# Fetch of edge rows written out with constant index addresses, three buffers, 41 turns beside one stage and 15 beside the next

## The reference, cut to what matters

```python
edge_index = stack([src, dst])
h = maximum(layernorm(x), 0);  x = x + L0(h, edge_index, W1, b1, W2, b2, W3, b3)   # three gcn layers 16-64-64-16
h = maximum(layernorm(x), 0);  x = x + L1(h, edge_index, ...)                      # 16-256-256, messages, 512-256-16
h = maximum(layernorm(x), 0);  x = x + L2(h, src, dst)                             # degree-scaled sum over edges
h = maximum(layernorm(x), 0);  x = x + L3(h, edge_attr_16, ...)                    # attention over edges

def L3(feat, efeat, W_msg, b_msg, W_attn, b_attn, src, dst):
    w_m = (efeat @ W_msg + b_msg).reshape(E, 16, 16)
    w_a = (efeat @ W_attn + b_attn).reshape(E, 16, 16)
    e1, e2 = w_m * feat[src][:, :, None], w_a * feat[src][:, :, None]
    attn = softmax of e2 over the edges of one target, for each of the 256 channels
    return segment_sum(e1 * attn, dst).sum(axis=1)
```

## Time and profile before

| | us |
|---|---|
| median of three runs | 3270.18 |
| profiled execution, its own time | 3269.55 |
| span of the profiled execution | 3267.7 |
| `layer0`, 745.5 to 1026.9 | 281.4 |
| `layer1_nodes`, 1026.9 to 1146.0 | 119.1 |
| `layer1_sum`, 1146.0 to 1385.5 | 239.5 |
| attention, from 1518 on | 1749 |

### The profile page before, as it was taken

How to read it: one execution, slowest core, us unless ns; L and a number is a source line. 1 busy time by engine, 2 the same in 40 slices (tenths; PEclk the granted TensorE clock), 3 DMA queues, 4 the chain that set the end, 5 groups by cost and what they waited for, 6 DMA issues and landing times. The chain is left out here.

```text
span 3267.7 us, 39524 instructions
## 1 busy us (share of the span) xinstructions
PE 2426.8 (74%) x7146; PEld 911.0 (28%) x7146; DVE 2494.0 (76%) x4298; ACT 1861.9 (57%) x7322; POOL 1358.8 (42%) x1220
## 2 busy tenths in 40 slices
PE   0888887785982689975688888888887888788740
PEld 0111111133551445533222222222222222222210
DVE  5999999943012445411699999999999999999977
ACT  2888888700000111110788788788878877887820
POOL 3000000006664400002676666666666766666503
PEclk8555556677975799987566766676677667667665
DMA  1000000002332554420122222222222222222113
GB/s 16 0 0 0 0 0 0 0 3 78 89 85 73 144 182 147 143 79 18 30 65 74 64 69 77 65 69 71 71 65 65 77 65 69 77 65 69 56 61 86
DMA packets 122244, 201.37 MB, mean 62 GB/s; under 512 B 55143, under 2 KB 76536, under 8 KB 116320
## 3 DMA queue, kind: packets, MB, share of 16 engines
q1 hardware_dynamic: 84192, 170.52, 15.0%
q0 software_dynamic: 38016, 30.45, 5.4%
HBM read 72.73 MB, written 128.17 MB: 61 GB/s over the span
## 5 line engine op out<-in xcount | busy, mean ns | idle before, releaser
L1463 POOL DMA_INDIRECT hs<-h_table,gix x880 | 1064.3, 1209 | 492.8 <-issue 265.7
L1555 ACT ACTIVATE e<-wps,hs 128x32 f32<-128x32 f32 x5632 | 1009.9, 590 | 201.1 <-PE wps L1487 160.0
L1487 PE MATMUL wps<-w_edge,ef 18*128 18x512 f32 x1760 | 729.7, 895 | 336.9 <-DVE e L1593 187.4
L1509 PE MATMUL slot_sums<-e,ident 128*128 128x512 f32 x1056 | 572.6, 700 | 9.7 <-DVE e L1658 9.7
L357 PE MATMUL acc<-q_hot,lo_hot 128*128 128x400 bf16 x1200 | 469.0, 495 | 132.8 <-DVE q_hot L327 70.3
L1487 PEld LDWEIGHTS wps<-w_edge,ef 18*128 18x128 f32 x1760 | 217.9, 248 | 812.9 <-DVE e L1593 337.2
L311 ACT ACTIVATE lo_hot<-lane,loT 128x128 bf16<-128x128 f32 x1200 | 353.7, 387 | 19.4 <-PE acc L357 19.2
L336 DVE TENSOR_TENSOR edges<-acc,edges 128x400 f32 x600 | 338.5, 564 | 22.6 <-PE acc L357 17.0
L1509 PEld LDWEIGHTS slot_sums<-e,ident 128*128 128x128 f32 x1056 | 230.6, 227 | 377.8 <-issue 367.3
L1593 DVE TENSOR_TENSOR e<-wps,hs 128x1024 f32<-128x1024 f32 (+1 forms) x220 | 314.6, 1430 | 26.9 <-PE wps L1487 26.9
L327 DVE TENSOR_SCALAR q_hot<-qcol,qT 128x400 bf16<-128x400 bf16 x1200 | 325.9, 313 | 5.3 <-issue 4.1
(11 more groups left out here) (305 smaller groups left out, 1979.8 us busy)
## 6 DMA issues: line engine op xcount, KB each, us to landing
rows_state<-states SPq DMA_DIRECT2D x44, 1280.0 KB, 4.6
rows_shift<-shifts SPq DMA_DIRECT2D x44, 640.0 KB, 3.0
edges_order<-got SPq DMA_DIRECT2D x56, 256.0 KB, 2.6
got_order<-edges_order SPq DMA_DIRECT2D x56, 256.0 KB, 2.9
ef_order<-efT SPq DMA_DIRECT2D x56, 256.0 KB, 3.0
hs<-h_table,gix POOLq DMA_INDIRECT x880
ef<-ef_order SPq DMA_DIRECT2D x44, 320.0 KB, 3.0
msg<-m_parts SPq DMA_DIRECT2D x10, 480.0 KB, 4.9
```

The lines of the kernel that those rows point to most:

```text
L1463: nc.gpsimd.indirect_dma_start(out=hs[u][:, s, :], out_offset=None, in_=d["h_table"], in_offset=bass.IndirectOffsetOnAxis(ap=gix[u][:, s:s ...
L1487: nc.tensor.matmul(wps[:, bank, :], ef[u][k:k + KM, g * P:(g + 1) * P], w[k:k + KM, :], start=True, stop=True).then_inc(a_mult, 1)
L1509: ins = nc.tensor.matmul(sums[:, (u + g) % 2, :], ident[:, :], e[u][:, g * SLOTS + c, :], start=(c == 0), stop=(c == SLOTS - 1))
L1555: ins = nc.scalar.mul(e[u][:, s, at], wps[:, bank, at], hs[u][:, s, f:f + 1])
```

## The change

The fetch counts single turns instead of pairs. `gather` and `store` take a Python number `n`, so that all 56 turns are written out. The gathers read their addresses directly from `start`; the tile `ix`, the copy into it and its two semaphores are gone. There are three buffers `got` with a semaphore pair each, turn `n` in buffer `n % 3`. 41 turns lie beside `layer0`, and 15 beside `layer1_nodes`, three in each of its five rounds. The loops of POOL (L684) and SP (L674) are gone.

```diff
-FETCH0 = GORDER // TURN // 2 - 5
+FETCH0 = GORDER // TURN - 15
...
+    TURNS = GORDER // TURN
+    RING = 3
...
-    def gather(self, pool, i, v):
-        nc = self.nc
-        nc.gpsimd.tensor_copy(self.ix[v][:, :], self.start[:, bass.ds(i * (2 * TURN) + v * TURN, TURN)]
-                              ).then_inc(self.y_idx, 1)
-        pool.wait_ge(self.y_idx, i * 2 + (v + 1))
-        pool.sem_inc(self.y_go, 1)
+    def gather(self, pool, n):
+        nc, v, k = self.nc, n % self.RING, n // self.RING
+        if k:
+            pool.wait_ge(self.gathered[v], 16 * TURN * k)
+            pool.wait_ge(self.stored[v], 16 * k)
         for g in range(TURN):
             nc.gpsimd.indirect_dma_start(
                 out=self.got[v][:, g, :], out_offset=None, in_=self.edge_rows,
-                in_offset=bass.IndirectOffsetOnAxis(ap=self.ix[v][:, g:g + 1], axis=0)).then_inc(self.gathered[v], 16)
+                in_offset=bass.IndirectOffsetOnAxis(ap=self.start[:, n * TURN + g:n * TURN + g + 1], axis=0)
+            ).then_inc(self.gathered[v], 16)
...
+    def store(self, sp, n):
+        v, k = n % self.RING, n // self.RING
+        sp.wait_ge(self.gathered[v], 16 * TURN * (k + 1))
+        sp.dma_start(self.edges_order[n * P:(n + 1) * P, :],
                      self.got[v][:, :, :].rearrange("p g n -> p (g n)")).then_inc(self.stored[v], 16)
...
-                with sp.Fori(0, FETCH0) as i:
-                    for v in range(2):
-                        fetch.store(sp, i, v)
+                for n in range(FETCH0):
+                    fetch.store(sp, n)
...
-                for v in range(2):
-                    fetch.gather(pool, 0, v)
-                with pool.Fori(1, FETCH0) as i:
-                    for v in range(2):
-                        fetch.gather_again(pool, i, v)
+                for n in range(FETCH0):
+                    fetch.gather(pool, n)
...
-                    for v in range(2):
-                        fetch.store(sp, FETCH0 + c, v)
+                    for v in range(3):
+                        fetch.store(sp, FETCH0 + 3 * c + v)
...
-                for c in range(ROUNDS):
-                    for v in range(2):
-                        fetch.gather_again(pool, FETCH0 + c, v)
+                for n in range(FETCH0, fetch.TURNS):
+                    fetch.gather(pool, n)
```

More of the change, by code:

```diff
@@ L418 @@
 class Fetch:
-    PAIRS = GORDER // TURN // 2
+    TURNS = GORDER // TURN
+    RING = 3
     def __init__(self, nc, ctx, io, keep, d, sem):
         self.nc, self.edge_rows, self.start, self.edges_order = nc, io["edge_rows"], keep["start"], d["edges_order"]
[L425 to L429, removed]
-    def gather(self, pool, i, v):
-        nc = self.nc
-        nc.gpsimd.tensor_copy(self.ix[v][:, :], self.start[:, bass.ds(i * (2 * TURN) + v * TURN, TURN)]
-                              ).then_inc(self.y_idx, 1)
-        pool.wait_ge(self.y_idx, i * 2 + (v + 1))
-        pool.sem_inc(self.y_go, 1)
+        self.got = [ctx.enter_context(nc.sbuf_tensor(f"got{v}", [P, TURN, SLOTS * KE], F32)) for v in range(self.RING)]
+        self.gathered = [sem(f"y_gather{v}") for v in range(self.RING)]
+        self.stored = [sem(f"y_stored{v}") for v in range(self.RING)]
+    def gather(self, pool, n):
[3 more added lines that the diff above has]
+            pool.wait_ge(self.stored[v], 16 * k)
         for g in range(TURN):
@@ L440, in gather, with wait_stored @@
                 out=self.got[v][:, g, :], out_offset=None, in_=self.edge_rows,
-                in_offset=bass.IndirectOffsetOnAxis(ap=self.ix[v][:, g:g + 1], axis=0)).then_inc(self.gathered[v], 16)
[L443 to L452, removed]
+                in_offset=bass.IndirectOffsetOnAxis(ap=self.start[:, n * TURN + g:n * TURN + g + 1], axis=0)
[4 more added lines that the diff above has]
+        sp.dma_start(self.edges_order[n * P:(n + 1) * P, :],
                      self.got[v][:, :, :].rearrange("p g n -> p (g n)")).then_inc(self.stored[v], 16)
-    def wait_stored(self, sp, pairs):
-        for v in range(2):
-            sp.wait_ge(self.stored[v], 16 * pairs)
+    def wait_stored(self, sp, turns):
+        for v in range(self.RING):
+            sp.wait_ge(self.stored[v], 16 * len(range(v, turns, self.RING)))
 def edge_groups(nc, io, keep, d, sem):
@@ L833, in _ @@
                                      parts[:, :, :, f * P:(f + 1) * P]).then_inc(n_dm, 16)
-                    for v in range(2):
-                        fetch.store(sp, FETCH0 + c, v)
+                    for v in range(3):
+                        fetch.store(sp, FETCH0 + 3 * c + v)
                 sp.wait_ge(n_dh, 16 * ROUNDS)
                 sp.wait_ge(n_dm, 32 * ROUNDS)
-                fetch.wait_stored(sp, fetch.PAIRS)
+                fetch.wait_stored(sp, fetch.TURNS)
             @block.gpsimd
             def _(pool):
-                for c in range(ROUNDS):
-                    for v in range(2):
-                        fetch.gather_again(pool, FETCH0 + c, v)
+                for n in range(FETCH0, fetch.TURNS):
+                    fetch.gather(pool, n)
             @block.tensor
```

## The result

| us | before | after | ratio, 95% interval |
|---|---|---|---|
| median, five runs each | 3271.28 (3267.5 to 3275.73) | 3235.63 (3233.88 to 3239.89) | 0.9892 (0.9878 to 0.9907) |
| profiled execution | 3269.55 | 3234.76 | |
| `layer0` | 281.35 | 237.91 | |
| `layer1_nodes` | 119.08 | 129.05 | |
| from `layer1_sum` on | 2121.7 | 2120.3 | |

The forecast was 3229. The span is 34.9 us shorter: -43.4 in `layer0`, +10.0 in `layer1_nodes`, -1.4 behind. The first term is the forecast one, the second is more than three times its size (+2.8 was forecast). That is the larger finding, and it comes last among the experiments.

A forecast was written before the change was run, and what follows sets the result against it. The fetch, on POOL's issue rate, was taken to hold `layer0` open for nearly 45 us. Profiled 3269.55 - 43.6 (`layer0`) + 2.8 (last round of `layer1_nodes`) = 3228.8, predicted 3229 us, range 3221 to 3238.

The forecast's parts named there:

- The first term: Border of `layer0` and `layer1_nodes`: DVE's idle time of 44.82 us becomes 1.23, so -43.6 us.
- the case that had 0.68: Whole kernel: the forecast holds as summed, 3224 to 3233 us; chance 0.68.
- the worst last round: Last round of `layer1_nodes`, upper bound: stretch 3.1 us and a slowly landing store, +6.8 us; total 3232.8.
- The copies go, five turns move: POOL in `layer0`: 0.75 us per turn saved, 164 gathers instead of 184, last gather ends at 960.6.
- DVE is late next, nothing else near: End of `layer0`: DVE's arithmetic is last at about 983.4, the fetch having 16.6 us to spare.
- The third buffer costs nothing in `layer0`: Fetch in `layer0`: a buffer has two turns, 10 us, to land, be stored and land again; costed at nothing.
- The last round, +2.8: Last round of `layer1_nodes`: twelve gathers instead of eight delay the third store, +2.8 us, bounds +0.6 and +6.8.
- The port rule: Last round of `layer1_nodes`: two two-input DVE passes could each hold a gather up to 1.49 us; term +4.0.
- The rounds keep their length: `layer1_nodes`: the sum allows no change in the rounds, which took 77.4 us from first to last.
- The rival on round lengths: `layer1_nodes`: clock changes make the rounds -7.7 or +2.6 us, total 3221.1 or 3231.4; chance 0.08 for over 4 us.
- The written-out list starves POOL: POOL in `layer0`: bringing in written-out gathers costs +0.6 us each, total 3311 us; chance of slower 0.04.
- the forecast of a faster kernel: Whole kernel: sign of the change, faster 0.95, same 0.01, slower 0.04.

The follow-up runs named there:

- e5: Changed kernel with two buffers instead of three; 3480.51 us in one run, on the chip where the kernel before takes 3345.8.
- e3: Changed kernel with 44 turns beside `layer0` and 3, 3, 3, 3, 0 in the rounds of `layer1_nodes`; 3228.93 us, before 3272.6 on that chip.
- e6: Changed kernel with the old split, 46 turns beside `layer0` and two per round; 3493.38 us, before 3345.8 on that chip.
- e7: Changed kernel with 44 turns beside `layer0`, then 3, 3, 3, 3, 0, without the last turn's gathers; 3456.16 us, ratio 1.048 to before.
- a_after_again: The changed kernel without any edit, timed again on the chip of 3298.2; 3449.75 us, ratio 1.0451 to the kernel before.
- e12: Changed kernel with copy, wait and increment per turn, 43 turns beside `layer0`, then 3, 3, 3, 4, 0, last turn's gathers omitted; 3287.79 us, ratio 0.9965 to before.
- e4: Changed kernel, each turn first copying its four addresses into a tile the gathers read, with a wait; 3236.31 us, before 3272.6 on that chip.
- e11: Changed kernel with each turn's address copy, the wait and a separate semaphore increment behind it put back; 3291.12 us, before 3298.2 on that chip.

## Why the prediction was right, and where not

The total was right by its range of 3221 to 3238, on the chip where it was measured. It lies outside the 3224 to 3233 of the case that had 0.68: the profiled execution got 34.8 us shorter where -40.8 was forecast. The first term carries the forecast. The terms of `layer1_nodes` were 7 us too small together, and 1.4 came back in the stages behind, which the sum took as unchanged. The total stayed in the range only because its upper bound lay 5 us above the worst last round, for the clock's spread; that part was luck.

- **The copies go, five turns move; -43.6 us.** Right: -43.4. POOL's busy time is 162.1 (forecast 162.5), the last gather ends at 957.95 (960.6). The 0.75 us per turn was the right size but not the copy's: the copy is 0.2 of it, and only copy and increment together make the rest. Taking both away at once hid that.
- **DVE is late next, nothing else near.** Right, with 0.53 us of idle time for the forecast 1.23; that its last sum ends 0.8 us later (982.93 for 982.15) offsets this. The third buffer costs nothing in `layer0`, and gives little there (e5).
- **The last round, +2.8.** The mechanism is right, the third store behind two, but the term is +6.1, near its upper bound of 6.8. Landing was taken as 4.3 us from round 1 and is 6.7 (+2.4): the last turn is padding, one address for all beside `msg` and two stores; a look at what `start` holds there would have told of the padding. The gathers start 1.65 us later against DVE than taken from before: the store that frees their buffer is issued 0.6 us earlier against DVE's round, but they start 6.9 us after it instead of 4.6. From the store to the next stage it is 2.7 us, not 3.5 (-0.8). The stretch, 1.24 + 0.55 = 1.8 us, is as forecast.
- **The port rule.** The gather beside L920 ends 0.81 us after it, the one beside L922 0.82 us after it (1099.28 - 1098.46); those beside the casts L919 and L921, with one input, keep their 0.94. A gather pays only what is left of the pass when it starts, so 1.8 us and not the 3.0 that two whole passes would make. The Trainium skill ("SBUF — State Buffer", shared port pair) says that whichever starts first gets the pair and the other blocks. For a gather that starts inside a pass the trace agrees. It shows nothing of the other direction: the gather at 1096.54 starts 0.43 us before L922 and keeps its 0.94, and L922 keeps its 1.49.
- **The rounds keep their length.** Not so: +3.1, and +0.7 before them. The rival on round lengths named such a shift (+2.6 for rounds of 20.0), but its 0.08 was for more than 4 us, and the sum took it as nothing. It belonged in the sum's bounds, since rounds of 17.4 to 20.8 us come in changing order.
- **The written-out list starves POOL.** Refuted: 164 gathers, 0.30 us between them, as the Trainium skill says of straight code ("Runtime: NRT & Kernel Launch", instruction fetch mechanics).
- **Moving five turns at all.** On a chip without the hold 44 turns end at 973.36 (e3). Two more at 5.0 us would end at 983.3, and 6.2 us on is 989.5, so the next stage would start 6.1 us later than the 983.5 measured. (The 977.99 of e6 is no measure of this: on its chip 41 turns end at 951.39, 6.6 us earlier than on the first, as DVE's work that stretches gathers hardly runs beside them.) By this estimate the move of five turns was worth 6.1 us in `layer0` and cost 6.1 at the end of the next stage, nothing in sum; e3, which moves two and puts none in the last round, has both.
- **What was missed.** I named slower cases only on POOL. The one that exists is on TensorE, which is held beside the faster gathers, on some chips. On the chip of 3298.2 the forecast of a faster kernel, given 0.95, is wrong by its sign. Nothing of it is to be seen in the first chip's profile of the kernel before, the only one taken.

Left open: what the holding is, why some chips have it, and whether the pause, the copy or the address tile relieves it. What the runs show is steps of 0.7 us, gathers beside dense matmuls, and 25 us until it ends. `layer0` of the kernel before was not profiled on such a chip, and e7's form was not timed on a chip without the holding.

## What to carry to other kernels

Where a stage ends with a helper engine's transfers, take pieces out of it only until the next engine is last: what is moved further costs in the place it goes to, and most in a last round, where nothing hides it. Ask of the last piece of a table whether it is padding, and leave it out or spread it. Count what a turn costs on the same chip and beside the same work as the kernel that it is compared with. A change that makes one engine run without a pause beside dense matmuls is to be timed on several chips, since a gain of 1.1% on one was a loss of 4.5% on another; with the old pace of 5.7 us a turn and the better split it was 0.35% ahead of before, on a third chip that shows the same gaps in the attention.

## What the runs showed of the hardware

- TensorE held to one matmul in 0.7 to 2.8 us in `layer0` on two chips (3345.8 and 3298.2) while indirect DMAs come every 1.25 us, and for 25 us after; not on those of 3271.3 and 3272.6, and not in `layer1_nodes`. On these two and on that of 3300.2 the attention has 60 to 68 us of gaps without a releaser among the products of the edge features (66.1 in a_after_again, 67.7 in e12).
- Four gathers of 128 x 512 bytes, all from one address and beside other transfers, have landed 6.7 us after the last of them instead of 2.8, at 69 GB/s with all DMA engines busy; with little beside them 3.5 us (e5).
- A gather that waits for a 0.2 us copy starts 0.27 us behind it (e4), and 0.81 us behind it with an increment between the wait and the gather (e11).
- A gather for 128 partitions takes POOL 0.94 us with 0.30 us between two, over 164 in a row; a gather that starts inside a DVE pass with two SBUF inputs ends 0.8 us after the pass.
